# Row maxima of the attention scores: added by extra operand rows instead of one-hot matmuls, in layers 0 to 2

## The reference, cut to what matters

```
scores = einsum('bhqd,bhkd->bhqk', q, k) * hd ** -0.5
attn   = softmax(scores, axis=-1)        # exp(s - max_k s) / sum
o      = einsum('bhqk,bhkd->bhqd', attn, v)
```

## Time and profile before

| what | value |
|---|---|
| median of 3 runs | 1548.19 us |
| profiled execution: its time, its span | 1548.05 us, 1546.1 us |
| TensorE matmul busy | 1410.9 us (91%) |
| VectorE busy | 1036.5 us (67%) |
| ScalarE busy | 779.5 us (50%) |
| GpSimd busy | 541.6 us (35%) |
| DMA packets, moved | 209129, 134.94 MB |
| matmuls at line 668, at line 672 | 2048 each |

### The profile page before, as it was taken

The page is one execution under the profiler, slowest core; times in us unless marked ns, Lnnn a source line. Parts: engine busy times, 40 slices in busy tenths (PEclk is TensorE's granted clock), DMA queues, the critical chain, the costliest instruction groups (busy, mean ns, idle before and its releaser), DMA issues. The chain is left out here.

```text
span 1546.1 us, 41104 instructions
## 1 busy us (share of the span) xinstructions
PE 1410.9 (91%) x16016; PEld 1055.9 (68%) x16016; DVE 1036.5 (67%) x2601; ACT 779.5 (50%) x1287; POOL 541.6 (35%) x739
## 2 busy tenths in 40 slices
PE   5799988999999998999999688877999799998998
PEld 2377676777777776777777566666776577776776
DVE  4698885666776677888447689897355466665342
ACT  2377664333323336676555366665544365555543
POOL 3355542211131304554323324433335134343222
PEclk9799999999999999999999899999999799999999
DMA  4765631111122123554001333453207576774011
GB/s 129 161 151 155 148 95 52 51 44 44 36 70 70 33 73 87 144 146 120 20 29 46 105 94 92 110 129 86 45 24 108 90 109 114 132 131 93 25 54 47
DMA packets 209129, 134.94 MB, mean 87 GB/s; under 512 B 142461, under 2 KB 191320, under 8 KB 202730
## 3 DMA queue, kind: packets, MB, share of 16 engines
q1 hardware_dynamic: 188978, 129.74, 35.3%
q10 hardware_dynamic: 19960, 2.57, 1.2%
HBM read 98.24 MB, written 33.24 MB: 85 GB/s over the span
## 5 line engine op out<-in xcount | busy, mean ns | idle before, releaser
L1546 DVE TENSOR_REDUCE negm<-banks 128x8 bf16<-128x1024 f32 x256 | 311.0, 1215 | 81.4 <-PE banks L650 79.6
L1235 ACT ACTIVATE prob<-banks 128x1024 f32<-128x1024 f32 x256 | 262.5, 1025 | 191.9 <-PE banks L672 191.1
L1363 ACT ACTIVATE hid<-banks 128x512 f32<-128x512 f32 x144 | 86.0, 597 | 220.3 <-PE banks L961 220.2
L1977 POOL TENSOR_TENSOR X<-X,gx 128x288 f32<-128x288 f32 x128 | 104.1, 826 | 255.0 <-DVE gx L1576 253.2
L977 PEld LDWEIGHTS banks<-wfc,hid 128*128 128x128 f32 x1152 | 156.6, 190 | 29.9 <-issue 20.3
L668 PE MATMUL banks<-qk 54*128 54x128 bf16 (+1 forms) x2048 | 168.7, 236 | 5.3 <-ACT prob L1235 5.0
L672 PE MATMUL banks<-mT,identb 64*128 64x128 bf16 x2048 | 165.7, 225 | 0.9 <-issue 0.9
L977 PE MATMUL banks<-wfc,hid 128*128 128x144 f32 x1152 | 161.1, 286 | 0.0
L650 PE MATMUL banks<-qk 54*128 54x128 bf16 (+1 forms) x2048 | 122.9, 241 | 39.6 <-DVE negm L1546 24.9
L960 PE MATMUL banks<-hT,wfc 128*128 128x512 f32 x288 | 149.6, 601 | 2.4 <-DMA wfc<-in_L_cond_w 2.4
L684 PE MATMUL banks<-prob,V 128*32 128x128 f32 x4096 | 143.5, 282 | 0.0
(11 more groups left out here) (169 smaller groups left out, 2777.0 us busy)
## 6 DMA issues: line engine op xcount, KB each, us to landing
qk<-qk_scr SPq DMA_DIRECT2D x96, 216.0 KB
gbuf<-gate_scr SPq DMA_DIRECT2D x64, 288.0 KB, 4.5
qk_scr<-parts SPq DMA_DIRECT2D x48, 288.0 KB, 2.8
qk<-qk_scr SPq DMA_DIRECT2D x96, 144.0 KB
qk<-cw_scr SPq DMA_DIRECT2D x8, 1024.0 KB, 4.9
qk_scr<-parts SPq DMA_DIRECT2D x48, 144.0 KB, 2.4
qk<-qk_scr SPq DMA_DIRECT2D x96, 72.0 KB
qk<-tok_scr SPq DMA_DIRECT2D x32, 216.0 KB
```

Source lines behind the costliest of these rows:

```text
L1235: act.activation(prob[:, 2 * (U % 3):2 * (U % 3) + 2, :], pairs[1][:], ACT.Exp, scale=scale).then_inc(a_exp, 1)
L1546: dve.tensor_reduce(negm[:, u // 2, :, 4 * (u % 2):4 * (u % 2) + 4], pairs[0][:].rearrange("q s (h k) -> q s h k", k=T), AX.X, ALU.max, ne ...
L1977: pool.tensor_tensor(x, x, gx[:, q, :, :], ALU.add).then_inc(g_x, 1)
```

## The change

In layers 0 to 2 the operands of the second scores get 8 more rows in each half, rows 54 to 61 (`RM = KS`). On the keys' side, row j is one over the tokens of head j's slot and zero over the others: a constant table from DRAM (`picking_rows`, 2 transfers of 8 rows for each buffer). On the queries' side, row j is head j's row of `mT`, repeated over the 8 slots, so the product adds to each head its own maximum. These rows are written for each pair by two transfers on ScalarE's queue (`row_of_maxima`), 8 rows by 8 slots by 128 bf16 each. The one-hot matmuls remain in layer 3 alone. `scores` waits, for each even unit, for the pair's two transfers instead of for `mT`.

```diff
-        def operand(l, side, n, U, s, i):
+        def operand(l, side, n, U, s, i, more=0):
-            rows = KS if l < 3 else KS + TB
+            rows = KS + more if l < 3 else KS + TB
...
         @block.sync
         def _(sp):
+            def picking_rows(r):
+                for s in range(2):
+                    row = 64 * s + RM
+                    sp.dma_start(qk[row:row + 8, 1, r].rearrange("j h t -> j (h t)").bitcast(F32), io.picks).then_inc(q_one[r], 16)
...
             sp.dma_start(X[:, 3 * G:4 * G, :], xv[:, 3 * G:4 * G, :]).then_inc(q_x[3], 16)
+
+            picking_rows(0)
+            picking_rows(1)
...
                     sp.wait_ge(s_mod, CR + L)
+                    if n == 1:
+                        picking_rows(2)
...
                     sp.wait_ge(d_hg, CR + NT * (1 if n == 8 else 8))
+                if n == 10:
+                    picking_rows(1)
...
                 pe.wait_ge(a_exp, CR + U)
-                pe.wait_ge(d_mt, CR + U // 2 + 1)
+                if l < 3:
+                    if u == 0 and n in (0, 1, 2, 10):
+                        pe.wait_ge(q_one[n % 3], 64 if n == 10 else 32)
+                    if u % 2 == 0:
+                        pe.wait_ge(q_m[U // 2 % 2], 32 * (U // 4 + 1))
+                else:
+                    pe.wait_ge(d_mt, CR + U // 2 + 1)
                 for i in range(4):
                     at = slice(T * i, T * i + T)
                     for s in range(2):
-                        pe.matmul(bank[2 + s][:, at], operand(l, 1, n, U, s, i), operand(l, 0, n, U, s, i),
-                                  start=True, stop=False)
-                    for s in range(2):
+                        mm = pe.matmul(bank[2 + s][:, at], operand(l, 1, n, U, s, i, 8), operand(l, 0, n, U, s, i, 8),
+                                       start=True, stop=l < 3)
+                    for s in range(2 if l == 3 else 0):
...
+            def row_of_maxima(P):
+                act.wait_ge(d_mt, CR + P + 1)
+                for s in range(2):
+                    row = 64 * s + RM
+                    act.dma_start(qk[row:row + 8, 0, P // G % 3, :, T * (P % G):T * (P % G) + T],
+                                  mT[64 * s:64 * s + 8, P % G, :].unsqueeze(1).to_broadcast([8, 8, T])) \
+                        .then_inc(q_m[P % 2], 16)
...
+                if l < 3:
+                    row_of_maxima(32 * l)
+                    row_of_maxima(32 * l + 1)
                 weights(l, 64 * l)
...
                         if U + 1 < last:
                             weights(l, U + 1)
+                        if l < 3 and u % 2 == 1 and U + 3 < last:
+                            row_of_maxima((U + 3) // 2)
                         if u % 2 == 1:
                             weighed_out(U // 2)
...
+    picks = np.repeat(np.eye(8, dtype=np.uint32) * 0x3F803F80, TG // 2, axis=1)
+    io.picks = put("picks", picks.view(np.float32))
```

More of the change, by code:

```diff
@@ L31 @@
 KS = 6 * D
+RM = KS
 TB = T // H
@@ L243, in build @@
         q_wq = [sem(f"q_wq{i}") for i in range(L - 1)]
+        q_one, q_m = [sem(f"q_one{r}") for r in range(3)], [sem("q_m0"), sem("q_m1")]
         q_gs, q_out = [sem(f"q_gs{l}") for l in range(L)], sem("q_out")
```

## The result

The median of the kernel after is 1666.84 us (4 runs, 1662.05 to 1668.88) against 1551.14 us (4 runs, 1546.15 to 1554.69) for the kernel before beside it: ratio 1.0744 with a 95% interval of 1.07 to 1.0787. It is 116 us slower. The forecast had the sign, but its 1590 us is 77 us short, and the time lies 37 us above the range.

A forecast was written before the change was run, and what follows sets the result against it. TensorE was taken to end most waits in layers 0 and 1, neither it nor VectorE alone in layer 2. 1548.05 - 25 (matmuls) + 53 (stalls) + 10 (clock) + 6 (starts) = 1592, named 1590 us; range 1521 to 1630.

The forecast's parts named there:

- waits on the rows in the stages: TensorE's second scores, layers 0 to 2: one stall a group, 4.8 us or 3.4 in layer 2; +81 before absorption.
- of them absorbed: Stalls fall beside waits TensorE had anyway: 1.2 us each in layers 0 and 1, 2 in layer 2; -28.
- lower clock after them: TensorE's matmuls run slower after idle time: +10 us, range 0 to +25.
- starts: Layer starts wait for turned maxima, copy and transfer: +2 us each, layer 0 more; +6 in all.
- ScalarE's issue, with its wait for `mT`: Two DMA issues a pair, 0.31 us each, between exponential and eviction; hidden, and nothing waits for maxima: 0.
- one-hot matmuls gone: Eight matmuls a unit leave TensorE in layers 0 to 2: 45 us of its time, -25 us counted.
- twelve stalls: One stall of TensorE for each of six groups in layers 0 and 1 each, 4.8 us long.
- 60 us at most: Cost of ScalarE's two issues a pair, 0.62 us over 96 pairs, if their cover were gone.
- The lower bound: Smallest gain expected from removing the one-hot matmuls: -10 us, with -45 at the other end.
- alternating with the reads, each waits for one packet of 8 KB: DMA engines serve two queues one for one; 16 pieces take 8.3 us, landing 9.6 us from issue.
- Rival (3): Two stalls a group, as delayed TensorE delays the next reads: +80, clock +25, 1634 us; chance 0.10.
- Rival (1): Rows land in time, in 2.6 us, if ScalarE's pieces go in one or two turns: 1526 us; chance 0.34.

The follow-up runs named there:

- ScalarE's wait alone: Kernel before plus picking rows and ScalarE's wait for each pair's maxima, with no transfers of maxima: 1557.07 us, 1.0024.
- paced reads: Changed kernel, with SyncE issuing a group's twelve reads by threes, each three only after the three before have landed: 1683.3 us, 1.0835.
- three placings: Kernel before plus transfers nobody waits for; both issues before the eviction 1572.68 us, both behind it 1576.84, one beside the exponential and one behind the eviction 1570.22.

## Why the prediction was wrong

The forecast had +44 us, the measurement +116. By the medians of the runs this is +22 (transfers that TensorE doesn't wait for), +98 (its wait), -4 (the matmuls; the intervals allow for none). Against the terms of the sum, with the stages' busy and idle time of above:

| step of the prediction | forecast | measured |
|---|---|---|
| waits on the rows in the stages | +81 | +83 |
| of them absorbed | -28 | -24 |
| lower clock after them | +10 | +30 |
| starts | +6 | +9 |
| ScalarE's issue, with its wait for `mT` | 0 | +22 |
| one-hot matmuls gone | -25 | -4 |
| sum | +44 | +116 |

So three steps failed, each by 20 us and all in one direction: clock, issue, gain. The first four measured rows are from one profiled execution of each of the two kernels that differ by the wait. They sum to 98 us, as the medians have it; the two executions differ by 94, because the rest of the program is 4 us shorter in the second. The last two rows are from medians.

**The clock: +10 was a third of it.** "If half of the twelve stalls bring about 3.5 us at half clock" took its size from one wait of 4.83 us, and left layer 2 and the shorter waits out. There were 31 waits in the stages, not 19, and the mean clock sank from 0.98 to 0.91 in layers 0 and 1. The same matmuls took 523.7 us instead of 493.8.

**ScalarE's issue: hidden by a number of another shape.** The prediction took 0.31 us from ScalarE's transfers of layer 3. These took

```profile
L1261 ACTq DMA_DIRECT2D qk<-mT x192: 695/696/1442, 62.2 to 1209.6; - x192
```

0.70 us each and 1.43 us a pair, longer than the exponential of 1.02 that was to cover them. Its price if that cover were gone, "60 us at most", was written down and then given no share of the sum. Of the 22 us some 5 are there with ScalarE's wait alone, which the prediction had at nothing as well. Already the slowest issue in the earlier trace rows, 611 ns, makes 1.22 us a pair. Nor was the eviction's 1.4 us of room, read in one unit, there in each: the eviction came late 41 times.

**The gain: -25 forecast, -10 alone, -4 in place.** The lower bound held. VectorE's and GpSimd's waits took over sooner, and layer 1, where TensorE was 92% busy, gave nothing; its clock fell there too, from 0.99 to 0.96. How much of the loss is the clock and how much the waits was not separated. With the rows' waits in place TensorE's busy time fell by 25.7 us, and 20.8 came back as idle time: it arrives sooner at a wait that ends when it ended before.

**The wait: the right sum by a wrong mechanism.** The prediction named the wait at the second scores on the DMA from `mT`, caused by the reads in front of it, and that heads the list. But "alternating with the reads, each waits for one packet of 8 KB" is wrong, although its landing, 9.6 us, is near the 9.3 us to the last piece of the longest wait in layer 1. The pieces don't alternate one for one: none passes for 3 to 6 us, until the reads issued before have been started, and packets of 1 KB leave that as it is. The earlier trace rows gave equal counts over 2.5 us, which say nothing of the order within them. The number of waits was wrong as well, mostly two pairs a group and not one, and each shorter, 2.7 us on average against 4.8 and 3.4. That the two errors cancel in the sum is luck. Rival (3), two stalls a group, had their number, and its 1634 was the nearest; the cause that it names (a late TensorE delays the reads) is not needed: a pair issued just behind a group's first reads and the pair after it are both within the 13 to 15 us that the reads take. Its 80 us for them also stood without a working beside the prediction's own bound of 95.

What fits is that the rows wait for the reads issued before them, by their amount: shorter reads free them, paced reads free them, smaller packets don't, and the packet records of two kernels show the order itself. Why two queues keep this order, and why GpSimd's keeps it only in part, no run here shows. The Trainium skill's rule that the prediction weighed ("DMA: Bandwidth & Descriptors", section "Queues, rings and completion order") is that an engine goes round its queues and drains a whole packet of descriptors from one before it switches. The trace doesn't agree with what the prediction made of it: by the earlier trace rows the three rows that a read of 27 gives an engine take 1.5 us, and two such turns are 3 us (an estimate), but the rows issued at 662.22 had no piece through by 668. A turn of so many descriptors should also be shorter with pieces of 1 KB, and the delay was not. Rival (1), which built on two turns, is excluded.

**Right, besides:** 62 rows cost no more than 54 (0.40 us in both lines of the timeline of TensorE above), the waits stand where reads are out, and the picking rows of SyncE are within the 5 us of the kernel with ScalarE's wait alone, which loads them too. The range stopped at 1630, below the terms' own upper ends (+95, +25, +60 for the issue): it was drawn from the cases and left out the one term that was priced but believed hidden.

## What to carry to other kernels

A small transfer that replaces cheap matmuls puts a DMA on the path of the engine that ends the stage: ask first what large transfers are issued before it, on another queue too, count its latency as the time that they still need, and charge the slower matmuls after each wait beside the wait (here 30 us on 60). Count the issue at its own shape, twice if there are two, and against the one instruction that covers it. And take the removed work out alone before anything else is built: here that would have shown 10 us to win, against 22 for the transfers before anything waits for them.

## What the runs showed of the hardware

- Transfers of 64 pieces of 256 B on a second queue, issued behind a group's reads (1.7 MB in 12 transfers) on the first, mostly had no piece through for 3 to 6 us, and then all within 1 to 4 us. They passed in about the order of issue across the two queues: behind 81 rows of 8 KB issued before, the first piece started when 81 to 90 had started, and the reads issued after a transfer did not hold its first piece back. On GpSimd's queue the first packets passed sooner (1.9 us) and the last ones as late. Free of reads they took 1.34 us to the first and 2.39 us to the last piece.
- The delay of the first piece was nearly the same with packets of 8 KB (3.3 us for the first pair of a group, 5 to 6 for the second) and of 1 KB (3.3 and 6.5), and the kernel before didn't mind packets of 1 KB either: 1.0024 [0.9998, 1.005].
- An issue on ScalarE took 0.70 us for 64 pieces over 8 partitions and 0.61 us (median, 0.50 to 1.71) for a single piece of 256 B: the pieces are the smaller part of it. On GpSimd 0.57 us for the 64.
- One issue a pair cost nothing that shows beside ScalarE's wait (1557.3 for 1557.07 us), two cost 20 to 25 us over the kernel before in three placings, the same within their intervals; unexplained.
- After 5.9 us idle TensorE's granted clock was 0.68 for the next 10 us, and 1.00 in the 8 us behind. Over three stages with 31 waits of 2.7 us on average the same matmuls took 6% longer.
